# A four-layer graph network on one core: the sync engine issues the first dense layer's weights after the 79th message step instead of the 8th

## The reference

```python
h = relu(layernorm(x)); x = x + relational_conv(h)       # 8 bases, 32 relations
h = relu(layernorm(x)); x = x + gcn_two_layers(h)
h = relu(layernorm(x)); x = x + equivariant_messages(h)   # per edge: gather, products, sum by node
h = relu(layernorm(x)); x = x + sage(tanh(sage(h)))       # agg @ W_l.T + h @ W_r.T + b, twice
```

## Time and profile before

| | us |
|---|---|
| median of 3 runs | 1455.31 (1454.26 to 1457.48) |
| profiled execution, own time | 1456.16 |
| its span, first to last instruction | 1454.3 |
| message steps 77, 78 and 81 begin on DVE | 1161.22, 1168.69, 1180.04 |
| SP issues `wa` | 1160.71 |
| first product with `wa` on PE | 1205.82 |

### The profile page before, as it was taken

One profiled execution on the slowest core, in us unless ns is written; L12 is line 12 of the kernel. 1 busy time (PEld: TensorE's weight loads), 2 busy tenths in 40 slices (PEclk: granted clock), 3 DMA queues, 4 the chain that ended last, 5 costly groups with the idle time before them and its releaser, 6 DMA issues. The chain is left out here.

```text
span 1454.3 us, 24122 instructions
## 1 busy us (share of the span) xinstructions
PE 1364.6 (94%) x6924; PEld 937.1 (64%) x6925; DVE 861.3 (59%) x2485; ACT 494.5 (34%) x1279; POOL 892.1 (61%) x927
## 2 busy tenths in 40 slices
PE   4888799999999999999999989998999979999998
PEld 2778788888885444444694866665666656686565
DVE  8778755555554667776433429988888854411111
ACT  7000000000005888882521235654555546311100
POOL 5777777777777777777777767777777720000000
PEclk9999999999999999999999989999999989999999
DMA  4678789888885652233211122222222330000000
GB/s 164 193 228 232 237 288 312 259 239 257 269 263 159 171 163 83 76 84 110 57 26 26 37 60 59 71 65 64 74 67 65 87 77 1 30 0 30 8 29 35
DMA packets 104166, 172.96 MB, mean 119 GB/s; under 512 B 20155, under 2 KB 54128, under 8 KB 104080
## 3 DMA queue, kind: packets, MB, share of 16 engines
q0 software_dynamic: 42832, 103.15, 24.2%
q10 hardware_dynamic: 27790, 39.30, 8.8%
q1 hardware_dynamic: 33458, 29.39, 6.5%
HBM read 153.74 MB, written 18.02 MB: 118 GB/s over the span
## 5 line engine op out<-in xcount | busy, mean ns | idle before, releaser
L874 POOL DMA_INDIRECT gath<-h_rows,idx x313 | 303.0, 968 | 95.0 <-issue 66.8
L1008 PEld LDWEIGHTS ps<-spread,gath 128*128 128x128 f32 x2504 | 306.9, 197 | 73.8 <-issue 43.4
L1008 PE MATMUL ps<-spread,gath 128*128 128x96 f32 x2504 | 313.0, 281 | 24.6 <-DMA gath<-h_rows,idx 17.7
L1030 PE MATMUL ps<-base_t,z 128*128 128x512 f32 (+1 forms) x640 | 308.4, 603 | 0.0
L930 POOL DMA_INDIRECT u<-u_rows,at x219 | 218.6, 998 | 66.8 <-issue 63.4
L1550 DVE TENSOR_TENSOR z<-z,ps 128x384 f32 x313 | 172.7, 552 | 100.1 <-PE ps L1008 88.5
L900 POOL DMA_INDIRECT slots<-att,idx_s x160 | 161.6, 1010 | 49.5 <-issue 47.6
L1221 PE MATMUL ps<-msg,hot 128*128 128x256 f32 x648 | 162.4, 394 | 20.6 <-DVE msg L1922 19.5
L900 POOL DMA_INDIRECT slots<-z,idx_s x153 | 153.5, 1003 | 43.9 <-issue 41.2
L1221 PEld LDWEIGHTS ps<-msg,hot 128*128 128x128 f32 x648 | 119.2, 192 | 81.0 <-DVE msg L1922 59.8
L1030 PEld LDWEIGHTS ps<-base_t,z 128*128 128x128 f32 (+1 forms) x640 | 107.3, 188 | 75.1 <-issue 74.9
(11 more groups left out here) (297 smaller groups left out, 1837.8 us busy)
## 6 DMA issues: line engine op xcount, KB each, us to landing
base_t<-in_bases_dram ACTq DMA_DIRECT2D x116, 256.0 KB
slots<-att SPq DMA_DIRECT2D x21, 256.0 KB, 5.2
at<-slots SPq DMA_DIRECT2D x21, 256.0 KB, 2.7
gath<-h_rows,idx POOLq DMA_INDIRECT x313, 4.2
u<-u_rows,at POOLq DMA_INDIRECT x219, 2.5
att<-in_attr_dram SPq DMA_DIRECT2D x40, 64.0 KB
slots<-att,idx_s POOLq DMA_INDIRECT x160
z<-in_attr_dram SPq DMA_DIRECT2D x39, 64.0 KB
```

The costliest lines, as they stand in the source:

```text
L874: nc.gpsimd.indirect_dma_start(out=gath[:, c % RING, :], out_offset=None, in_=h_rows, in_offset=bass.IndirectOffsetOnAxis(ap=idx[:, par, c ...
L1008: last = mm(bank[:, k * SPREAD:(k + 1) * SPREAD], gath[:, h_slot, k * P:(k + 1) * P], s_of.rearrange("p b d -> p (b d)"), start=True, stop ...
L1030: return mm(ps[BANKS[n]][0:rows(n), :], z[:, k, b, n * P:n * P + rows(n)], base_t[:, k, :], start=(t == JOINS[n]), stop=(t == JOINS[n] + T ...
```

## The change

The wait ahead of the loads asks for 79 finished message steps (`STEPS - 2`) in place of 8. Nothing else differs: the same four DMAs in the same place of SP's stream.

```diff
             sp.wait_ge(out_ok, AGG[2])
-            sp.wait_ge(m_ok, RING)
+            sp.wait_ge(m_ok, STEPS - 2)
             for t, w in ((wa, s_w1l), (wb, s_w1r)):
                 sp.dma_start(t[:, :, :], w.rearrange("(k p) f -> p k f", p=P)).then_inc(ld_w3, 16)
             sp.dma_start(b_a[:, 0:KIN], s_b1).then_inc(ld_w3, 16)
```

## The result

The changed kernel takes 1459.02 us in the median of 11 runs (1457.42 to 1462.92), the kernel before 1455.3 in the median of 11 (1454.26 to 1463.55). The ratio is 1.0029 with a 95% interval of 1.0018 to 1.004: 4.2 us slower, 2.6 to 5.8. The forecast had 1457.5 and a range of 1453.0 to 1460.3.

A forecast was written before the change was run, and what follows sets the result against it. The prediction took the message steps as paced by POOL's gather issue, with one 3.7 us stall from the loads. Late step 81 (+0.8) and PE's clock (+1.4) gave +2.2 us on 1455.31: 1457.5 us, range 1453.0 to 1460.3.

The forecast's parts named there:

- The old wait never bound and the new one does: SP ahead of `wa`: old condition held nothing back; new one delays `wa` from 1160.71 to 1171.9, 11.2 us later.
- The stall goes from step 78 and returns at step 81: DVE message steps: the 3.7 us gather stall leaves step 78; `wa`, 1.8 us ahead of the last gather, stalls step 81.
- The present stall is worth less at the end than where it stands: End of the message steps: without any collision step 81 starts at 1177.9, 2.1 us earlier, less than the stall's 3.7.
- Term 1: Start of step 81 on DVE: 1180.8 in place of 1180.04, held by late gathers; +0.8 us (-0.2 to +1.4).
- Term 2: PE's clock falls in 5.6 us idle ahead of step 81's sums: L1221 +1.1, L1248 +0.3; +1.4 us (0 to +1.9).
- The chain behind: The ten blocks after the message steps: move as a whole, unchanged, with 1 us either way kept for the half-clock stretch.
- Deadline of the loads: Last load lands at about 1182.2, PE first reads `wa` at 1205.82: 23 us of cover, cost nothing.
- First rival: Step 81's gathers pass the loads, by shared queues or late `m_ok`: step 81 at 1177.9, -2.1 us, 1453.2; chance 0.22.
- Second rival: Clearly slower: gathers and `wb` hinder more, three gathers caught, lower clock through L1248 into first blocks; +5.4 us, 1460.7; chance 0.17.
- Signs: Expected in the profile: `wa` at 1172, step 78 idle under 1 us, step 81 4 or more, L1221 about 3.1 us.
- the forecast's own range: Whole kernel, if the main forecast of 1457.5 us holds: 1455.8 to 1459.2 us, chance 0.58.

The follow-up runs named there:

- small kernels: Three stand-alone kernels rebuilding only gathers, loads, DVE and PE steps, phases varying load place and row repetition; last step starts 3.0 to 8.4 us behind its last gather's issue.
- the runs at 2046 us: Whole-kernel experiments while the kernel before itself took 2045 to 2066 us; the changed kernel there: 2059.99 us against 2054.25, ratio 1.0009 (0.997 to 1.0048).

## Why the prediction was right in kind and small in size

- The old wait never bound and the new one does: right. `wa` goes out at 1174.08, 12 us behind the last small load; less the 2.2 us by which this profile is late anyway, that is the 1171.9 of the forecast, and 1.8 us ahead of the last gather, as forecast.
- The stall goes from step 78 and returns at step 81, and ends with the gather, not with ACT: right, with 5.07 us of idle time.
- The present stall is worth less at the end than where it stands: right in kind. The 2.1 us that the prediction gave it there are not borne out. In the small kernels a last step with the repeated row and no load starts 5.0 to 5.4 us behind its last gather's issue; by that, step 81 of the kernel before, at 5.9, lost 0.5 to 0.9 us, or up to 1.4 with the late issue of that gather (my estimate). With five steps left the small kernel lost nothing (4.5 us against 5.2), with two left 2.7, but its steps repay faster than the real ones.
- Term 1, +0.8 us, was mis-sized; it is 1.8. The step that failed is "POOL's queue stood still until 4.8 us after the issue of `wa`", "so until 1176.7". I took the standstill of step 78, where the gathers before it were quick. Here `wa` moved only from 1178 on, 4 us behind its issue, while a slow gather of step 81 was under way; the last gathers then waited until 1180.5, 6.4 us behind it. That is 1.6 us more than I had; from there to the start of step 81 it took 3.6 us, and I had 4.1. That the slow gather is what held `wa` is read from the order of the rows and was not tested in the whole kernel. I had noted the gathers' slowness and used it only for their own time, not for how they push the load, and with it the end of the standstill, back.
- Term 2, +1.4 us, is 2.0: L1221 grew by 1.8 where I took 1.1 from the earlier trace rows, since nearly all of it and not half lies at the lower level, and L1248 by 0.2. The small kernel shows the term by itself. The prediction called the slow matmuls behind the old stall hidden or repaid. Not quite: in the kernel before step 80 waits 0.96 us on DVE for ACT's copy L732 of PE's L1197, and step 81 0.40 for L723, so a part of the present stall's remainder may be PE's.

```profile
1177.81 0.56 DVE L1913 TENSOR_TENSOR msg<-py,u 128x384 f32<-128x384 f32 x1 [0.96 <-ACT py L732]
```

- The chain behind, left as it is: 0.5 us slower, inside the 1 us kept for it.
- Deadline of the loads: 25 us of cover (forecast 23), cost nothing, as forecast.
- First rival (the gathers pass the loads): refuted by the profile and by the small kernels. The rule of the Trainium skill that stood beside it ("DMA: Bandwidth & Descriptors", "Queues, rings and completion order") was read too narrowly in the prediction. The page has an engine change queues at packets of its own kind, bundles of 9 to 17 descriptors as a rule and 64 at most. The profile's packets carry 2 KB here (538 for 1.08 MB), and 34 of them passed on each engine with none of POOL's. So the rows exclude a change at every packet of the profile. If such a packet is one descriptor, they also speak against bundles of 17, but not against bundles of 64.
- Second rival (clearly slower): two parts of it came true, the mutual hindrance and the whole L1221 at the lower clock, and the result lies between the forecast and it. Its third part did not: the 64 packets behind 1180.5 are two gathers, not three.
- Signs: in the 3.5 us behind the last gather's issue POOL's queue was to show hardly a packet. It still had 30, with 0.06 MB; the empty stretch came later, from 1178 on.
- Chances: 1459.02 lies just inside the forecast's own range (to 1459.2). By the 2.9 us that the prediction took as the least that can be told, 4.2 is slower, to which it gave 0.28, and not the same, to which it gave 0.64.

Sum: 0.8 + 1.4 = 2.2 forecast, 1.8 + 2.0 + 0.5 = 4.3 in the profiles, 4.2 in the runs. All three parts came out longer than forecast, none made up for another. What stays open: the interval of the runs at 2046 us is wider than the effect, so no whole kernel has shown that undoing the collision gains the time back; and what makes the whole kernel take 2046 us at one time and 1455 at another.

## What to carry to other kernels

A big load that shares the DMA engines with small gathers that steps wait for should be issued where steps are left to repay the stall, or behind the last gather, not two or three steps ahead of the end of a stage. Look for the last gather in the timeline. How many steps a stall of some 4 us needs hangs on what each repays: in the small kernel, at 1.2 us each, four or five left 0.5 us or nothing of it; at 0.7 us each, as here, it takes more (my estimate from 3.7 us and 0.67 a step: six). A wait that a later condition creates can cost twice where the engine behind it is PE: once as idle time, and, where the wait falls in one piece ahead of the last matmuls, once more as matmuls at half clock (5.49 us in place of 2.75).

## What the runs showed that I had not expected

- Gathers of one repeated row: 0.44 us a packet against 0.11 for spread rows. In the small kernels without loads the last step starts 5.0 to 5.4 us behind the last gather's issue, against 3.0. Padding costs some 2 us at the end of such a stage. Spread row numbers, written once into the tile that fills the slots, bring the packets back to 0.11 us; the time that this gains was not seen.
- A load among slow gathers is late too: `wa` needed 8.0 us to land, not 5.9.
- Cutting 2 MB into eight DMAs, all issued within 4 us, hardly helps the gathers (0.3 to 0.5 us).
- The same kernel took 2046 us and 1459 us on one chip at different times. In the profiles of the slower time engines sit idle for up to 26 us at a time for nothing that the profile shows.
